# Three transformer layers behind a rotation: other hand-written orders on four engines, and more useless products on TensorE

## What is computed

```python
U, _ = jnp.linalg.qr(P)                       # P 144 x 64
R = expm(A)                                   # A skew 64 x 64, from the condition
x = x + einsum('btd,nd->btn', z @ R - z, U)   # z = x @ U
for layer in (1, 2, 3):                       # 16 heads of 9
    h = modulate(norm(x), shift_msa, scale_msa)
    q, k, v = split(h @ W_qkv + b_qkv)        # layer 3: q and k rms-normed per head
    x = x + gate_msa * (softmax(q k^T / 3) v @ W_proj + b_proj)
    h = modulate(norm(x), shift_mlp, scale_mlp)
    x = x + gate_mlp * (gelu(h @ W_fc1 + b_fc1) @ W_fc2 + b_fc2)   # 576 wide
```

## Time and profile before

| | us |
|---|---|
| median of 3 runs | 368.15 (368.13 to 370.33) |
| the profiled execution | 366.48 |
| its span, first to last instruction | 364.7 |
| PE, DVE, ACT, POOL busy | 304.6, 293.6, 207.4, 166.1 |
| mean granted clock of TensorE | 0.934 |

### The profile page before, as it was taken

The page is one execution under the profiler, slowest core; times in us unless marked ns, Lnnn a source line. Parts: engine busy times, 40 slices in busy tenths (PEclk is TensorE's granted clock), DMA queues, the critical chain, the costliest instruction groups (busy, mean ns, idle before and its releaser), DMA issues.

```text
span 364.7 us, 10730 instructions
## 1 busy us (share of the span) xinstructions
PE 304.6 (84%) x3474; PEld 211.6 (58%) x3478; DVE 293.6 (80%) x1511; ACT 207.4 (57%) x460; POOL 166.1 (46%) x536
## 2 busy tenths in 40 slices
PE   1969964981748888799999999999898989989896
PEld 0924821570125355477878777777666666766675
DVE  4999999999994678878888888797989887887632
ACT  4146110252002355788888888887786876768552
POOL 5424332457543322535454645444746555462442
PEclk9999565898678999999999999999999998999999
DMA  4697300049200223241222222222120223222101
GB/s 145 190 247 233 123 1 0 4 86 308 89 1 0 47 44 74 44 59 36 58 44 45 47 47 46 45 45 46 29 44 18 47 45 45 43 32 45 34 18 34
DMA packets 49503, 23.58 MB, mean 65 GB/s; under 512 B 40954, under 2 KB 47966, under 8 KB 49320
## 3 DMA queue, kind: packets, MB, share of 16 engines
q1 hardware_dynamic: 49448, 22.89, 27.1%
HBM read 12.82 MB, written 0.62 MB: 37 GB/s over the span
## 4 chain that ended last, share of the span: by engine, by line
PE 43%; DVE 36%; issue 8%; DMA 4%; POOL 3%; SPq 3%; ACT 1%; POOLq 0%; DVEq 0%
PE ps L1017 36%; DVE grow L1643 4%; DVE nmax L1972 3%; DVE top L1698 3%; DVE trow L1643 3%; DMA skw_r<-brief 3%; PE ps L1411 3%; DVE beta L1677 2%; DVE den L1683 2%; DVE tfac L1691 2%; DVE late L1665 2%; DMA tmask<-in_tmask 2%; DVE lead L1665 1%; PE ps L1308 1%; DVE skw_r L2021 1%
## 5 line engine op out<-in xcount | busy, mean ns | idle before, releaser
L1972 DVE TENSOR_REDUCE nmax<-ps 128x4 f32<-128x512 f32 x96 | 63.4, 684 | 12.2 <-PE ps L1017 12.0
L797 ACT ACTIVATE skw_t<-ps 128x512 f32<-128x512 f32 x96 | 52.0, 595 | 15.3 <-PE ps L1017 14.7
L449 POOL TENSOR_TENSOR root<-grow,half 32x1 f32<-32x1 f32 x64 | 34.6, 542 | 53.6 <-DVE grow L1643 53.2
L1017 PE MATMUL ps<-skw_r 54*128 54x128 bf16 x768 | 43.6, 218 | 5.4 <-issue 2.0
L1017 PEld LDWEIGHTS ps<-skw_r 54*128 54x128 bf16 x768 | 30.8, 94 | 21.1 <-issue 16.1
L1017 PE MATMUL ps<-mT_t,fc1w_t 128*128 128x256 f32 (+1 forms) x130 | 36.0, 379 | 0.0
L1017 PE MATMUL ps<-fc2w,skw_r 128*128 128x144 f32 (+1 forms) x240 | 34.7, 292 | 0.0
L1017 PEld LDWEIGHTS ps<-fc2w,skw_r 128*128 128x128 f32 (+1 forms) x240 | 30.8, 190 | 1.6 <-issue 0.2
L1017 PE MATMUL ps<-sel,identb 128*128 128x512 bf16 x63 | 18.8, 423 | 12.0 <-DVE grow L1643 10.9
L1017 PE MATMUL ps<-nmT,sel 64*128 64x128 bf16 x384 | 28.0, 218 | 0.0
L814 ACT ACT_TABLE_LOAD x21 | 26.9, 1283 | 0.4
(11 more groups left out here) (273 smaller groups left out, 817.8 us busy)
## 6 DMA issues: line engine op xcount, KB each, us to landing
gmod<-spread_mods SPq DMA_DIRECT2D x3, 1408.0 KB, 13.2
adaw_t<-in_ada SPq DMA_DIRECT2D x3, 432.0 KB
tails<-in_tail SPq DMA_DIRECT2D x3, 427.1 KB
skw_r<-brief SPq DMA_TRANSPOSE x72, 2.5
skw_t<-in_skw SPq DMA_DIRECT2D x1, 1024.0 KB
fc1w_t<-in_fc SPq DMA_DIRECT2D x3, 320.0 KB
fc2w<-in_fc SPq DMA_DIRECT2D x3, 288.0 KB
qkvw_t<-in_qkv SPq DMA_DIRECT2D x3, 216.0 KB
```

What stands on the lines that cost most here:

```text
L449: g.tensor_tensor(root[:, p, j:j + 1], grow[:, i % 4, 0:1], half[:], ALU.pow).then_inc(root_ready, 1)
L797: a.activation(prob[g].rearrange("p i t -> p (i t)"), ps[:, 2 + g % 2, :], ACT.Exp, scale=SCALE).then_inc(prob_ready, 1)
L1017: return pe.matmul(o, lhsT, rhs, start=start, stop=stop, skip_group_check=True)
L1972: d.tensor_reduce(nmax[:, v % 2, first:first + 7:2], ps[:, 6 + g % 2, :].rearrange("p (i t) -> p i t", i=4), AX_X, ALU.max, negate=True).t ...
```

## The change

The change does four things.

1. `WARM_AT` is range(54, 64) instead of range(54, 62): three products that nobody reads also behind pivots 62 and 63.
2. `AWAKE_AT` is new: in visits 15, 17, 19 and 21 max_turn first does three such products, 128x512 into bank 6, which need three of that visit's maxima to be read.
3. All branches of the slot loops of POOL, ACT, PE and DVE have new orders, and some steps another slot: attention_add one slot later (slot - 3), first_tail one later, inverse_norms at slot, second_deviation at lag 4, the second part of fc1 in the odd slot ahead of parts_turn (lag 5), last_deviation at slot - 3, last_out at slot - 4.
4. Nothing is changed in the steps themselves, or in SP's queue.

```diff
-WARM_AT = range(54, 62)
+WARM_AT = range(54, 64)
 LEFT_BANKS = (6, 7, 5)
 LATE = 2
+AWAKE_AT = range(2 * B - 1, VISITS - 1, 2)
...
             def max_turn(v):
+                if v in AWAKE_AT:
+                    o = refill(6, max_ready, 4 * v + 3)
+                    for r in range(3):
+                        mm(o, identb[:], sel[:, 4 * r:4 * r + 4, :])
                 o = refill(7, nmT_ready, v + 1).bitcast(BF16)
                 pe.wait_ge(nmp_ready, v + 1)
...
                     pair_at(mlp_out, slot, 5)
                     visit_at(max_high, slot)
+                    visit_at(max_low, slot)
                     visit_at(residue, slot + 1, start=1)
-                    visit_at(max_low, slot)
```

More of the change, by code:

```diff
@@ L606, in _ @@
                     visit_at(first_deviation, slot + 2, start=2)
                     pair_at(mlp_add, slot, 6)
[L608 to L612, removed]
+                elif slot >= VISITS - 1 and slot % 2 == 1:
+                    visit_at(inverse_norms, slot, start=2 * B)
+                    visit_at(first_tail, slot + 1, start=2)
@@ L632, in _ @@
                 elif (slot + 1) // B == 2 and slot % 2 == 0:
+                    visit_at(attention_add, slot - 3)
+                    visit_at(inverse_norms, slot, start=2 * B)
+                    visit_at(first_tail, slot + 1, start=2)
+                    pair_at(second_deviation, slot, 4)
                     pair_at(mlp_add, slot, 6)
@@ L1436, in _ @@
                 if slot < 2 and slot % 2 == 0:
-                    pair_at(fc1, slot, 4, 0)
-                    visit_at(qkv, slot + 1, start=1)
+                    visit_at(max_turn, slot - 1)
+                    pair_at(h2_turn, slot, 4)
+                    visit_at(scores_T, slot - 1, 0)
+                    visit_at(parts_turn, slot)
+                    visit_at(pv, slot - 1, 0)
+                    visit_at(qkv, slot + 1, start=1)
+                    visit_at(pv, slot - 1, 1)
+                    visit_at(scores, slot, 0)
@@ L1439, in _ @@
                     visit_at(pv, slot - 1, 0)
                     visit_at(pv, slot - 1, 1)
+                    visit_at(scores, slot, 2)
+                    visit_at(pv, slot - 1, 2)
+                    visit_at(last_fc1_main, slot - 3, start=LAST)
+                    visit_at(h_turn, slot + 1, start=2)
+                    visit_at(pv, slot - 1, 3)
+                    visit_at(last_tail_turn, slot - 3, start=LAST)
+                    visit_at(qkv, slot + 1, start=1)
+                    visit_at(last_turn, slot - 2, start=LAST)
@@ L1441, in _ @@
+                    pair_at(fc2, slot, 5, 1)
+                    visit_at(last_fc1_tail, slot - 3, start=LAST)
+                elif (slot + 1) // B == 2 and slot % 2 == 0:
                     visit_at(max_turn, slot - 1)
@@ L1562, in _ @@
                     visit_at(h_turn, slot + 1, start=2)
-                    visit_at(parts_turn, slot)
                     visit_at(scores_T, slot - 1, 0)
@@ L2118, in _ @@
                     visit_at(maxima, slot, 0)
                     visit_at(maxima, slot, 1)
+                    visit_at(residue, slot + 1, start=1)
+                    visit_at(input_means, slot + 3, start=2)
                     visit_at(input_squares, slot + 3, start=2)
+                    visit_at(maxima, slot, 2)
+                    visit_at(maxima, slot, 3)
+                    visit_at(second_parts, slot + 1, start=1)
+                    visit_at(max_high, slot)
+                    visit_at(max_low, slot)
```

495 lines of the change are left out of this document (237 added, 258 removed).

## The result

| | before | after |
|---|---|---|
| median of 18 runs each | 369.31 us (366.20 to 372.03) | 372.09 us (370.32 to 375.07) |
| ratio after / before, 95% interval | | 1.0086 (1.0060 to 1.0112) |
| profiled execution | 366.48 us | 373.69 us |
| span | 364.7 us | 371.8 us |
| mean granted clock | 0.934 | 0.936 |

The change makes the kernel slower by 0.9%. I had forecast 365.8 us, 0.7 us under the profiled execution of before, so the sign is wrong and the time lies outside the range. So the 7.2 us between them is read by stages, and what counts is what other kernels repeat.

The account below looks back on a forecast made before the run. TensorE full in layers one and two, a chain through TensorE and VectorE in layer three, idle TensorE also lowering the clock. 366.48 - 0.3 + 0.4 + 0.5 - 1.65 + 0 + 0.4 = 365.8 us, range 362.8 to 369.8.

Parts of the forecast that it names:

- start of layer one: parts_turn(0) ahead of six useless products and qkv(1) makes TensorE wait: +0.4 us, bounds 0 and +1.5.
- the wrong ones: Signs against the forecast: layer two pairs under 17.5, layer three pairs under 20, or granted clock 0.50 after 119.
- Pivots: Batches at pivots 62 and 63 fill idle TensorE and may hold the clock to 111.7: -0.3 us.
- the bound "0": Pivots, worse end: the clock falls at 104.9 all the same and the batches cost nothing; other end -0.75 us.
- rival (b): Clock falls at layer one's start behind idle TensorE, price 1.6 to 3.4 us: 369.5 us, slower, chance 0.15.
- Layers one and two: New order adds changes between product kinds on a full TensorE: +0.1 us per pair, +0.5 in all, bounds -1 to +2.
- the 0.2 that I set against it: Layers one and two: a wait of about 0.2 us before o_turn goes, offsetting the split of attention products.
- Layer three, useless products: Three products inside max_turn's wait in four visits hold the clock: -1.65 us, bounds 0 to twice that against slower runs.
- Layer three, order: max_low, o_back, third_parts and others move; pluses and minuses are alike: 0 us, bounds -1 and +1.
- the prediction's first case: Layer three: mlp_add starts first, max_low ends 0.27 us earlier; if max_low starts first, 0.87 earlier.
- ScalarE and GpSimd: New places for ACT's PSUM-emptying steps and POOL's inverse_norms, hidden by PE or the DMAs: costed at nothing.
- Tail: last_turn(22) ahead of visit 23's last attention products waits for DVE's ln: +0.4 us, bounds 0 and +1.

Follow-up runs that it names:

- g2: Kernel before with the change's useless products (pivots 62 and 63; visits 15, 17, 19, 21), no tiny products, old orders: 368.49 us, ratio 0.9970.
- e6: Changed kernel plus 60 tiny products on TensorE ahead of the last pivots: 371.03 us, ratio 1.0106.
- e10: Kernel before, old orders, with both kinds of the change's useless products and 54 tiny products ahead of the last pivots: 362.87 us, ratio 0.9867.
- e1: Kernel before with WARM_AT = range(54, 64) and nothing else: 370.30 us, ratio 1.0053.
- e4: Changed kernel without the three useless products in visits 15, 17, 19 and 21 (AWAKE_AT empty): 372.85 us, ratio 1.0141.
- e7: Changed kernel with fc2's second half again ahead of all attention products in odd slots of layers one and two: 371.17 us, ratio 1.0104.
- g3: Kernel before with the useless products at pivots 62 and 63 and 54 tiny ones, none in layer three: 364.72 us, ratio 0.9889.
- g4: Changed kernel with visit 23's last attention products ahead of last_turn(22) again: 371.89 us, ratio 1.0090.
- e2: Kernel before with parts_turn(0) moved ahead of qkv(1) and its six useless products, nothing else: 369.99 us, ratio 1.0085.
- e11: Changed kernel with TensorE's and VectorE's layer three branches as before, fc1's second part staying in the odd slot: 373.24 us, ratio 1.0136.
- e3: Changed kernel with WARM_AT back at range(54, 62) and qkv(1) back ahead of parts_turn(0): 371.06 us, ratio 1.0103.
- e8: Kernel before with max_low ahead of residue in the odd slots of layer three, nothing else: 367.80 us, ratio 1.0012.
- e5: Kernel before plus 60 tiny products (120 TensorE instructions) ahead of the last pivots: 366.36 us, ratio 0.9944.

## Why the prediction was wrong, point by point

Two comparisons set the new orders against the old ones with the same useless products. After against g2 has no tiny products on either side; the ratios, 1.0086 and 0.9970, are 1.2% apart, the profiled executions 5.0 us (373.69 and 368.71), and the clock falls at 109.2 or 109.3 in both. e6 against e10 has tiny products on both sides, 60 and 54, so e6's layers begin twelve TensorE instructions later, as many as moved a packet in e1. Their ratios, 1.0106 and 0.9867, are 2.4% apart, the profiled executions 8.3 us (371.15 and 362.85), and the clock holds at the pivots in e10 alone. The profiles cut at the same places (differences from unrounded times):

| stretch | e6, new orders | e10, old orders | e6 less e10 | after less g2 | after less before | term predicted |
|---|---|---|---|---|---|---|
| to h_turn(0) | 114.9 | 114.1 | +0.9 | -0.1 | +0.9 | -0.3 |
| h_turn(0) to max_turn(0) | 17.2 | 14.4 | +2.9 | +3.0 | +2.0 | +0.4 |
| max_turn(0) to (3) | 21.2 | 20.4 | +0.8 | +0.8 | +1.1 | in the same |
| (3) to (13) | 89.1 | 88.1 | +1.0 | +0.8 | +1.7 | +0.5 |
| (13) to (15) | 19.3 | 20.0 | -0.7 | -0.7 | -0.7 | |
| (15) to (21) | 64.6 | 63.1 | +1.4 | +0.3 | +0.6 | 0, and -1.65 for the fall |
| (21) to (23) | 19.9 | 18.7 | +1.3 | +0.1 | +0.8 | in the same |
| (23) to the end | 23.2 | 22.3 | +0.9 | +0.8 | +0.8 | +0.4 |

The start of layer one is the largest term, +3.0 us where +0.4 stood, and there both comparisons agree. The first row shows the fall at the pivots, not the orders, since all of these kernels but before have the batches. The step into layer three, (13) to (15), is shorter by 0.7 us in the new orders; no term stood for it, and why was not looked into. Of the signs named, one of the wrong ones came: a granted clock of 0.50 behind 119, at 122.8.

*Pivots.* Right in the mechanism, wrong in holding it to be safe. Where the clock holds (e1, e4, e7, e10, g3, g4) h_turn(0) stands at 114.1 to 114.2, 0.8 to 1.0 us sooner than the 115.0 of before: about the 0.75 of the prediction. In the other seven kernels with the batches it falls at 109.2 to 111.3 instead, on the products that lie on the path: h_turn(0) at 114.7 to 115.1 with the short fall, 115.9 to 116.0 with the long one, as in the profile of after. Which of the two a kernel shows is not set by an edit: e4, e7 and g4 change nothing ahead of the layers, and their clock holds. The step that failed is the bound "0": I took the fall as either there at 104.9 or gone, and not as moved to a dearer place. The term measured is between -1.0 and +1.0, and +0.9 in the profile of after.

*Start of layer one.* This is the failed step that I had written down as rival (b). The term +0.4 assumed that the clock holds. Eight of the nine kernels with both the swap and the two batches have a stretch at 0.50 that begins between 120.3 and 123.0, and none of the eight kernels without the swap has. Swap and fall together cost 2.9 to 3.0 us up to max_turn(0) (2.0 against before), not 0.4, and the visits behind give none of it back. The two kernels with the swap whose profile has no fall there, g4 and e2, have 15.98 and 15.71 us where after has 17.28, so the fall is 1.3 to 1.6 of it. The chance of 0.15 was too low: the idle 2.6 us ahead of 122.55 are longer than the 1.65 us behind which the clock had fallen in the earlier trace rows. But the length of the wait does not decide alone: around a wait of 2.32 us the clock fell in e4, e7 and e11, and around one of 2.31 or 2.32 it held in g4 and e2.

A second fall had no term at all. In four of the ten kernels with the new orders (e3, e4, e7, e11) a stretch at 0.50 begins between 144.9 and 151.1, in none of the eight with the old ones; in three of the four max_turn(0) to (3) takes 23.0 to 23.3 us, elsewhere 21.2 to 22.1 in the new orders. That is part of why taking the start back (e3) does not bring the time back.

*Layers one and two.* The mechanism was right, the size of a pair was too small: +0.22 us, not +0.1, of which PE's own busy time is 0.18. Splitting pv costs 0.14 (e7), less than the 0.2 of the earlier trace rows; what failed is the 0.2 that I set against it for the wait before o_turn, which gave nothing back, since the pair was full.

*Layer three, useless products.* Right in kind. In the old order five of six profiles without them show one or two falls there (all but e1), in kernels with them there is none in visits 15 to 21; g3 against e10 has two falls and 3.3 us between the profiled executions, so 1.6 each, as predicted; in the new orders e4 has one fall and a ratio 0.55% (2 us) over the changed kernel's. But over all executions of e10 and g3 the ratios are only 0.2% apart (0.9889, 0.9867), with intervals that overlap, so the term's size is shown by profiles alone.

*Layer three, order.* The step that failed is "pluses and minuses are alike, I take 0": the new order costs 0.5, 0.7, 0.2 and 1.3 us in the four pairs between e10 and e6, but 0.3 in all four together between g2 and after. What goes with the difference is the landings, which I had named as what closes the chain. In the old order they count: from max_turn(15) to max_turn(23) g2 and e1, with all eight visits late, take 83.7 and 82.7 us, and e10, with one at 5.9, takes 81.8; all three hold the clock there. In the new order they don't: after has late landings in all eight visits and takes 84.0 us, e6 has three and takes 84.5. So the new order does not gain what the old one gains when its landings are on time. Which step of it is to blame stays open.

max_low's place, for which a gain of up to 0.87 was open, was tried only with mlp_add in front (e8): max_turn comes 0.28 us sooner against max_high, the 0.27 of the prediction's first case, residue 0.8 later, and the time is the same within 0.3% faster and 0.5% slower. The Trainium skill's rule (SBUF — State Buffer, "Who interferes with whom"), by which the order of issue decides who blocks, agrees in all eight slots: 0.17 or 0.18 us ahead of mlp_add in two of after, 0.79 behind its start in the other two and in the four of e8. What the 0.87 would be worth stays open.

*ScalarE and GpSimd.* Their new places were put at nothing. No run changes them alone, so whether that holds is not shown.

*Tail.* +0.8 to +0.9 instead of +0.4, and 0.55 of it is the place that the prediction named (g4).

*What I had not seen.* The old order depends on where the instruction packets fall: e1 lost 18.15 + 18.72 + 18.21 - 3 x 17.60 = 2.3 us in layer two by twelve more instructions of TensorE, e5 gained 0.6% by 120. No term stood for it, and what it moves is as large as the whole change.

*The sum's base.* It starts from the profiled 366.48, while the limits of 1% (364.5 and 371.8) go by the median of 368.15, and 18 runs put that median at 369.31; so the forecast and the limits were 1.7 us apart from the start. Rival (b) was priced up to 370.7, and half of its chance was then put over 371.8, which its own price does not reach. It is the rival that came nearest, and 372.09 lies over its price too, since the layers and the tail lost beside it.

## What to carry to other kernels

Useless products that hold the clock pay only when they hold it up to the next dense stretch; a batch that only moves the fall can put it on the path. Where a product is moved ahead of others and must wait, price the idle time twice, by the wait and by a fall behind it. And before an order is judged by less than 1%, time it with the instruction stream shifted once or twice: here that alone moved the time as much as the change did (g2 to e10, 0.9970 to 0.9867).

## What the runs showed of the hardware that I had not expected

In the layers the DMA trace has a packet of 0.02 MB on the queue of kind instruction, q8, every 9.5 to 10.1 us on average (4.6 to 21.5 apart, in before, after, e1, e6 and e10), about one per 250 TensorE instructions; it takes 0.9 to 1.6 us. If it falls among a transposing DMA's packets, one share of that DMA often lands 1.5 to 2.9 us behind the other fifteen, or all shares of it land late, and the DMAs behind it come later too: 5.1 us from third_parts to the last landing become 5.6 to 7.5. Not every late landing has such a packet: visit 10 lands after 5.8 us in before without one. Its place moves with the number of TensorE instructions ahead (e1, e5), so adding or removing instructions in one stage changes waits in another. That the packet carries TensorE's instructions is inferred from this, and not shown in another way.
